# Sixteen pairs in three buffers, TensorE's products placed by time per slot, GpSimd's sums spaced, and the chunk loop written out

## The reference, cut to what matters

```python
xc, z = jnp.split(jnp.einsum('bld,ed->ble', x, W_in), 2, axis=-1)
u = silu(conv1d(xc, w_c) + b_c)                                  # 1024 channels, 4 taps
dt, Bm, Cm = jnp.split(jnp.einsum('bld,ed->ble', u, W_x), [32, 48], axis=-1)
delta = softplus(jnp.einsum('blr,dr->bld', dt, W_dt) + b_dt)
A = -jnp.exp(A_log)                                              # 1024 x 16
h[t] = exp(delta[t] * A) * h[t-1] + delta[t] * Bm[t] * u[t]      # 16 states per channel
y[t] = (h[t] * Cm[t]).sum(states) + u[t] * Dp
out = jnp.einsum('bld,od->blo', y * silu(z), W_out)
```

## Time and profile before

| | us |
|---|---|
| median of 3 runs | 8613.19 (8611.42 to 8617.14) |
| the profiled execution | 8617.45 |
| its span, first to last instruction | 8615.6 |
| first scan of chunk 0 | 238.9 |
| last scan's end | 7757.2 |

### The profile page before, as it was taken

How to read it: one execution, slowest core, us unless ns; L and a number is a source line. 1 busy time by engine, 2 the same in 40 slices (tenths; PEclk the granted TensorE clock), 3 DMA queues, 4 the chain that set the end, 5 groups by cost and what they waited for, 6 DMA issues and landing times. The chain is left out here.

```text
span 8615.6 us, 126403 instructions
## 1 busy us (share of the span) xinstructions
PE 7396.0 (86%) x31688; PEld 4113.0 (48%) x31688; DVE 7620.8 (88%) x8802; ACT 5873.9 (68%) x10702; POOL 6574.0 (76%) x2826
## 2 busy tenths in 40 slices
PE   5788888888888888888888888888888888876886
PEld 3444444444444444444444444444444444445753
DVE  2899999999999999999999999999999999995717
ACT  5777777777777777777777767777777777754415
POOL 0888888888888888888888888888888888881103
...
GB/s 197 49 51 50 46 50 51 51 51 52 53 51 47 51 52 49 45 63 61 61 51 52 51 52 46 51 51 48 46 50 51 51 52 50 47 37 153 166 127 148
DMA packets 223573, 552.99 MB, mean 64 GB/s; under 512 B 26272, under 2 KB 26528, under 8 KB 201824
## 3 DMA queue, kind: packets, MB, share of 16 engines
...
## 5 line engine op out<-in xcount | busy, mean ns | idle before, releaser
L931 POOL TENSOR_TENSOR bu<-w,b_rep 128x1024 f32<-128x1024 f32 x2048 | 4808.6, 2361 | 956.0 <-DVE h L1007 955.9
L1007 DVE TENSOR_TENSOR_SCAN h<-decay,h_last,bu 128x512 f32<-128x512 f32 x3840 | 4817.3, 1271 | 200.1 <-PE turn L519 140.6
L728 ACT ACTIVATE decay<-delta,neg_a 128x512 f32<-128x512 f32 x4096 | 2802.7, 689 | 1862.4 <-DVE h L1007 1848.1
L519 PEld LDWEIGHTS turn<-ident_m,h 128*128 128x128 f32 x16384 | 1918.4, 143 | 3163.2 <-DVE acc L1027 1246.1
L519 PE MATMUL turn<-ident_m,h 128*128 128x128 f32 x16384 | 2591.6, 282 | 615.3 <-DVE acc L1027 359.3
L1027 DVE SCALAR_TENSOR_TENSOR acc<-turn,c_now,acc 128x512 f32<-128x512 f32 x3200 | 2327.5, 727 | 191.9 <-PE turn L519 185.8
L448 PE MATMUL proj<-conv_in,conv_diag 128*128 128x512 f32 x2048 | 1039.7, 596 | 45.7 <-ACT halo L662 45.7
L448 PE MATMUL proj<-x_conv,w_in 128*128 128x512 f32 x2048 | 1055.5, 613 | 22.0 <-DMA x_conv<-xt 17.0
L448 PE MATMUL proj<-x_gate,w_in 128*128 128x512 f32 x2048 | 1034.2, 597 | 43.1 <-ACT stage L718 29.5
L448 PE MATMUL proj<-zy,w_out 128*128 128x512 f32 x2048 | 1033.7, 599 | 0.9 <-DVE zy L1036 0.9
L946 POOL TENSOR_TENSOR acc_v<-acc_v,prod 128x1024 f32<-128x1024 f32 x320 | 755.2, 2360 | 16.7 <-ACT prod L742 16.7
...
## 6 DMA issues: line engine op xcount, KB each, us to landing
b_rep<-b_rows SPq DMA_DIRECT2D x1024, 256.0 KB, 3.3
...
xt<-stage ACTq DMA_DIRECT2D x128, 256.0 KB, 2.4
...
```

What stands on the lines that cost most here:

```text
L519: mm = pe.transpose(out[:, b * P:(b + 1) * P], h[:, k % 2, b, j * P:(j + 1) * P], ident[:])
L728: act.activation(decay[:, b, :], delta[:, blk, :], ACT.Exp, scale=neg_a[:, n, blk:blk + 1]).then_inc(decay_set, 1)
L931: pool.tensor_tensor(bu[:, s // 2 % 4, :, :], w[:, blk:blk + 2, :], b_rep[:, k % 4, :].unsqueeze(1).to_broadcast([P, 2, T]), ALU.mult).the ...
L1007: dve.tensor_tensor_scan(h[:, k % 2, b, :], decay[:, b, :], bu[:, s // 2 % 4, b % 2, :], start, ALU.mult, ALU.add).then_inc(scanned, 1)
```

## The change

What it does, part by part:

- All 16 pairs go by ScalarE and GpSimd, in three buffers of `prod`. The buffer of the first pair of a half is the running total, so `acc_v` is gone. The first product of pair q waits for GpSimd's addition of the pair that had its buffer, in most cases q - 2.
- The products are laid out by time: each slot has the same total of weights, turn tiles included (state 0.55, skip 1.05, product 1, x_proj 1.1, delta 1.25). That is about 1.3 products in a slot with one state tile.
- The skip tiles move from slots 0 to 3 and 32 to 35 to slots 4, 5, 6, 7 and 30, 33, 36, 39, and the second half's y tiles from 20, 22, 24, 26 to 22, 24, 26, 28. `PROD_LAG` is 2 instead of 3.
- A Silu is moved to a position (`silu_at`) where no product follows it for some slots. The pieces between it and its half's last copy stay in list order.
- GpSimd's four sums and four products for `delta` and `w` stand at fixed positions 17, 21, 25, 29, 49, 53, 57, 61. Before, each product stood one position behind its sum.
- The loops over chunks become Python loops: every chunk is written out.

The diff, cut to its core:

```diff
-         ("conv", 7, 0), ("out", 0, 0), ("x_proj", 0, 0), ("turn_c", 0, 0), ("out", 1, 0), ("delta_next", 0, 0), ("out", 2, 0),
-         ("delta_next", 1, 0), ("out", 3, 0), ("delta_next", 2, 0), ("gate", 0, 0), ("delta_next", 3, 0)] + [
-         ("gate", b, 0) for b in range(1, NB)]
+         ("conv", 6, 0), ("conv", 7, 0), ("out", 0, 0), ("x_proj", 0, 0), ("turn_c", 0, 0), ("out", 1, 0), ("delta_next", 0, 0),
+         ("delta_next", 1, 0), ("out", 2, 0), ("delta_next", 2, 0), ("delta_next", 3, 0), ("out", 3, 0)] + [
+         ("gate", b, 0) for b in range(NB)]
-RATE = 1.17
-TAKE_LAG, TAPS_LEAD, W_LAG, X_PROJ_LAG, XDBL_LAG, CONV_LAG, PROD_LAG = 4, 2, 10, 5, 3, 4, 3
+TAKE_LAG, TAPS_LEAD, XDBL_LAG, CONV_LAG, PROD_LAG = 4, 2, 4, 4, 2
+W_AT = {17: ("sum", 2), 21: ("product", 2), 25: ("sum", 3), 29: ("product", 3),
+        49: ("sum_next", 0), 53: ("product_next", 0), 57: ("sum_next", 1), 61: ("product_next", 1)}
+Y_AT = ((116, 118, 120, 122), (22, 24, 26, 28))
+SKIP_AT = ((7, 4, 5, 6), (30, 33, 36, 39))
+WEIGHT = {"x_proj": 1.1, "delta": 1.25, "delta_next": 1.25, "turn_c": 0.5, "state": 0.55, "skip": 1.05, "y": 0.55}
+def silu_at(end):
+    at = end + TAKE_LAG
+    behind = (at - PROD_LAG - 5) % (2 * J)
+    return at if behind < 5 else at + 2 * J - behind
 def timetable():
-    at, end_of = 0.0, {}
+    room = [-sum(WEIGHT[tile[0]] for tile in tiles_at) for tiles_at in TURN_AT]
+    whole = sum(PRODUCTS[kind] * WEIGHT.get(kind, 1.0) for kind, _, _ in ORDER) - sum(room)
+    room = [r + whole / (SLOTS_BODY - 3) for r in room]
+    slot, left, end_of = 0, room[0], {}
...
-        slots = [int(at + q / RATE) for q in range(PRODUCTS[kind])]
-        at += PRODUCTS[kind] / RATE
+        slots = []
+        for q in range(PRODUCTS[kind]):
+            while left < WEIGHT.get(kind, 1.0) / 2 or slot < earliest:
+                slot += 1
+                left = min(left, 1.0) + room[slot]
+            slots.append(slot)
+            left -= WEIGHT.get(kind, 1.0)
...
-V_PAIRS = [q for q in range(GROUPS // 2) if q % HALF_Q != 2]
-V_SET = {q: i % 2 for i, q in enumerate(V_PAIRS)}
+V_BUFFER = (0, 1, 2, 1, 2, 1, 2, 1, 2, 1, 0, 1, 0, 1, 0, 1)
+def emptied_before(q):
+    old = max(o for o in range(-len(V_BUFFER), q) if V_BUFFER[o] == V_BUFFER[q])
+    pair = old % len(V_BUFFER)
+    return ("join", pair // HALF_Q) if pair % HALF_Q == 0 else ("pair", pair), old < 0
...
-        with eng.Fori(start + 1, end) as G:
+        for G in range(start + 1, end):
             run(G, Kind(layer))
...
-    prod = sb("prod", [P, 2, 2, HB * P])
-    acc_v = sb("acc_v", [P, 2, HB * P])
+    prod = sb("prod", [P, 3, 2, HB * P])
...
-            more = prod[:, 1 - V_SET[q]] if q % HALF_Q == 1 else acc_v[:]
-            pool.tensor_tensor(acc_v[:], more, prod[:, V_SET[q]], ALU.add).then_inc(vsum_set, 1)
+            total = prod[:, V_BUFFER[q - q % HALF_Q]]
+            pool.tensor_tensor(total, total, prod[:, V_BUFFER[q]], ALU.add).then_inc(vsum_set, 1)
```

More of the change, by code:

```diff
@@ L107 @@
+LAST_SKIP = [("skip", hf, SKIP_AT[hf].index(max(SKIP_AT[hf]))) for hf in range(2)]
 TURNS = 2
@@ L125, in turn_tiles, with timetable @@
     return order, carried
 TURN_AT, CARRIED = turn_tiles()
+WEIGHT = {"x_proj": 1.1, "delta": 1.25, "delta_next": 1.25, "turn_c": 0.5, "state": 0.55, "skip": 1.05, "y": 0.55}
[3 more added lines that the diff above has]
+    return at if behind < 5 else at + 2 * J - behind
+def timetable():
+    room = [-sum(WEIGHT[tile[0]] for tile in tiles_at) for tiles_at in TURN_AT]
+    whole = sum(PRODUCTS[kind] * WEIGHT.get(kind, 1.0) for kind, _, _ in ORDER) - sum(room)
+    room = [r + whole / (SLOTS_BODY - 3) for r in room]
+    slot, left, end_of = 0, room[0], {}
+    work, take = [[] for _ in range(SLOTS_BODY)], [[] for _ in range(2 * SLOTS_BODY)]
+    for i, (kind, x, earliest) in enumerate(ORDER):
+        if kind == "conv":
+            earliest = end_of["conv_half", x] + CONV_LAG
+        if kind == "x_proj":
+            earliest = silu_at(end_of["conv", NB - 1]) + 1
+        if kind in ("turn_c", "delta_next"):
+            earliest = end_of["x_proj", 0] + XDBL_LAG
+        slots = []
[5 more added lines that the diff above has]
+            left -= WEIGHT.get(kind, 1.0)
+        for at in sorted(set(slots)):
+            lo = slots.index(at)
+            work[at].append((kind, x, i, lo, lo + slots.count(at)))
+        end = end_of[kind, x] = slots[-1]
+        if kind == "conv_half":
+            take[end + TAKE_LAG - TAPS_LEAD].append(("taps", x, i))
+        take[end + TAKE_LAG].append((kind, x, i))
+        if kind.startswith("delta") and x % 2 == 1:
+            for q, part in enumerate(("exp", "ln")):
+                take[end + TAKE_LAG + 1 + q].append((part + kind[5:], x // 2, i))
+        if kind == "conv" and x % HB == HB - 1:
+            take[silu_at(end)].append(("silu_u", x // HB, i))
+        if kind == "gate" and x % HB == HB - 1:
+            take[silu_at(end)].append(("silu_z", x // HB, i))
+    return work, take, end_of
@@ L129, with tiles @@
+WORK, TAKE, END_OF = timetable()
+def tiles(first, last):
+    kept = [i for i, (kind, _, _) in enumerate(ORDER) if not (first and kind in NOT_FIRST or last and kind in NOT_LAST)]
+    return {i: n for n, i in enumerate(kept)}, len(kept)
+PROJ_TILES, PROJ_FIRST = tiles(False, False)[1], tiles(True, False)[1]
+PROJ_PROLOGUE = 2 * NB + 1 + 1 + HB
 V_AT = (0, 3)
 HALF_Q = STATES // 2
-V_PAIRS = [q for q in range(GROUPS // 2) if q % HALF_Q != 2]
-V_SET = {q: i % 2 for i, q in enumerate(V_PAIRS)}
+SUM_LAG_Q = 11
@@ L135, in by_act @@
+V_BUFFER = (0, 1, 2, 1, 2, 1, 2, 1, 2, 1, 0, 1, 0, 1, 0, 1)
 def by_act(tile):
[L136 to L143 removed]
+    return tile[0] == "skip" or tile[0] == "state" and tile[2] == V_AT[tile[1] % 2]
+def emptied_before(q):
+    old = max(o for o in range(-len(V_BUFFER), q) if V_BUFFER[o] == V_BUFFER[q])
+    pair = old % len(V_BUFFER)
+    return ("join", pair // HALF_Q) if pair % HALF_Q == 0 else ("pair", pair), old < 0
@@ L432, in _ @@
             body(start, Kind(layer, at_start=True))
-            with sp.Fori(start + 1, end - 1) as G:
+            for G in range(start + 1, end - 1):
                 body(G, Kind(layer))
@@ L737, in product @@
                 act.wait_ge(c_set, 2 * G + (k // HALF_C + 1))
-            of_last, reader = reader_before(q)
-            if k % 2 == 0 and not (kind.first and of_last):
-                act.wait_ge(vsum_set, sum_base(G, kind) + (kind.sums.index(reader) + 1 + C_PROD))
-            act.activation(prod[:, V_SET[q], k % 2, :], turn[:, BANK[tile], :], ACT.Copy,
+            emptied, in_last = emptied_before(q)
+            if k % 2 == 0 and not (kind.first and in_last):
+                behind = in_last and emptied not in SUMS_CARRIED
+                at = SUMS.index(emptied) - len(SUMS) if behind else kind.sums.index(emptied)
+                act.wait_ge(vsum_set, sum_base(G, kind) + (at + 1 + C_PROD))
+            act.activation(prod[:, V_BUFFER[q], k % 2, :], turn[:, BANK[tile], :], ACT.Copy,
                            scale=c_now[:, j, n:n + 1]).then_inc(v_done, 1)
@@ L969, in body @@
             for p in range(PAIRS):
-                for what, pair in W_AT[p]:
-                    if kind.has(what.replace("sum", "delta").replace("product", "delta")):
-                        delta_w(G, what, pair)
+                what, pair = W_AT.get(p, ("", 0))
+                if what and kind.has(what.replace("sum", "delta").replace("product", "delta")):
+                    delta_w(G, what, pair)
                 k, pr = divmod(p, 2)
```

74 lines of the change are left out of this document (16 added, 58 removed).

## The result

The kernel became slower, not faster: 8828.72 us (median of 4 runs, 8821.29 to 8832.35) against 8615.08 of the kernel before (4 runs, 8611.42 to 8617.14). The ratio is 1.0247, with a 95% interval from 1.0230 to 1.0265. I had forecast 8427 and a range from 8300 to 8535. The profiled execution took 8832.35 us.

A forecast was written before the change was run, and what follows sets the result against it. VectorE was taken as the engine with least room, busy 222.6 us per chunk. New chunk: 220.0 busy + 9.4 idle = 229.4 against 235.3; with the end chunks 187 us less than 8617.4, or 8427 as median; range 8300 to 8535.

The forecast's parts named there:

- The rival of the emptied buffer: ScalarE's product waits for GpSimd to empty its buffer, 14.4 us more idle per chunk; 8859 us, chance 0.05.
- its margin at 3.3 less a lag of 1.9: GpSimd's addition frees a buffer 3.3 us before ScalarE's product needs it, less GpSimd's lag of 1.9: no wait.
- Position 119: silu_z stands ahead of gate 4's copy ... 1.2: At position 119 silu_z delays gate 4's copy, so gate 6 starts late and scan 120 waits 1.2 us.
- a halved clock: Within the TensorE-bound rival: product-free slots 75 to 77 halve the clock, up to 3 us a chunk; centre 8585, chance 0.08.
- a low clock in mid-chunk: Sign that the forecast is wrong: TensorE's granted clock falls in the middle of a chunk; no size given.
- 0.87 us: TensorE's price for one product of two passes, used throughout the slot-by-slot walk.
- both ring waits: Slots 84 to 88 and 92 to 96: delta_next pieces hold the two proj banks, delaying out 2 and out 3; 1.9 us each.
- The list of stalls: Slot-by-slot walk of VectorE's waits in a chunk of the new order, summing to 9.9 us.
- its upper bound of 15 idle: VectorE's idle per chunk could reach 15 us if the late tiles knock on.
- 29 us by my rows: Chunk edges: writing out the loop gains nothing in layer 1 and 2.1 us in 14 chunks of layer 2.
- hardly a stall: Rival: the new order leaves VectorE idle only 1 to 6 us per chunk, centre 3.5; 8247 us, chance 0.13.
- the new order does nothing: Rival: old stalls only move, idle stays 11.4 us per chunk; 8487 us, inside the forecast's range, no separate chance.

The follow-up runs named there:

- deltas apart: Changed kernel with the four delta_next pieces back in their old places, an out between each two; 8758.04 us.
- both back: Changed kernel with the first half's Silu of z back at position 116 and the delta_next pieces in their old places; 8582.88 us.
- skips spaced: As both back, but skip tiles moved to slots 1, 4, 5, 6 and 33, 37, 41, 45; 8592.73 us.
- The filled gap: Changed kernel with one more product, which nobody reads, in each of slots 75, 76 and 77 of chunks 1 to 30; 8765.89 us.
- Silu_z back: Changed kernel with the first half's Silu of z at position 116 instead of 119; 8642.01 us.
- looped: Changed kernel with the hardware loops over chunks restored; 8880.75 us.
- pairs and loop: Kernel before with sixteen pairs in three buffers and its loops written out, all else old; 8516.64 us.
- the best version: As skips spaced, with x_proj's copy and turn_c two earlier and every proj piece taken three slots after its last product, not four; 8417.06 us.

## Why the prediction was wrong

**Right: the pairs, and for the changed kernel the buffers and GpSimd.** Alone, the pairs brought 8617.87 to 8536.95, 81 us where the sum had 30 x 2.6 = 78. ScalarE's products never wait for GpSimd in the changed kernel (waits after), and the spacing changed nothing that can be told. The rival of the emptied buffer, which gave 8859 and so came nearest to the measured time, was wrong in its mechanism for this kernel: the loss has another cause. But that the wait is nothing held only behind the other stalls. In deltas apart, both back and skips spaced, where VectorE is faster from slot 86 on, it is there, 91 or 92 times in an execution, up to 2.5 us long and 191, 142 and 141 us in all. I had put its margin at 3.3 less a lag of 1.9.

**The step that failed: "Position 119: silu_z stands ahead of gate 4's copy ... 1.2".** I followed what the moved Silu delays on ScalarE and in the `proj` ring, and did not ask who reads its result. The y tile's gate product at slot 116 does (one Silu covers all four blocks of the half), and it was 4.0 us too early for it. TensorE, left without work by the same wait, then ran at half clock, which made 2.5 of the 1.2 at slot 120. Moving this one step back is worth 187 us of the 402 between forecast and result. The 402 are 375 in chunks 1 to 30 (12.5 each), 21 in the two end chunks and 5 outside the chunks.

**The second error: the clock as a rival, at one place.** I gave a halved clock 0.08, at slots 75 to 77, and named a low clock in mid-chunk as a sign that I am wrong; the sign came. It falls there, and at four other places: where a ring wait leaves TensorE short of work (86, 94), behind the Silu wait (117), and in the stretch of slots 22 to 28, where y tiles take the place of products (25). In the last one the stall of slot 26 comes and goes with it: in chunks 16 to 22 the clock stays up there and the stall is absent. I had priced every product behind a wait at 0.87 us; several cost twice that, and 0.5 + 1.4 us became 1.60 + 3.11. The filled gap shows that a low clock costs in this way (63 us in all, 1.6 per chunk at the two places themselves); for slots 86 and 94 the deltas edit took away the ring wait and the low clock together (59 to 71 us). How they share it is seen where the clock stays up behind the same ring wait: 1.8 us instead of 4.7 at slots 94 to 96 (chunk 22 after), and 1.12 + 0.64 = 1.8 instead of 2.7 at slots 86 to 88 (chunk 6 of Silu_z back). So both ring waits were priced about right, at 1.9 each, and the term that failed there is the 0.87 us per product, which left no room for a lower clock.

**The list of stalls** was otherwise a fair guide: at slots 6, 8, 28, 32, 38, 40, 43, 48, 87 and 88 each lies within 0.3 of its forecast, 7.9 us measured for 6.8 forecast. The 87 is in part luck: I had its products at full clock, and four passes took 2.94 us there. The sum failed by what it left out, and its upper bound of 15 idle held only late tiles, not a reader too early or a slower clock.

**The loop** was 29 us by my rows; it is 14 in the old order and 52 in the new one. Rows of a looped kernel can't price an edge for another order: in the old one the stalls at the edge shrank by 1.7 us a chunk, and 1.3 of them came back at slots 62 to 64 with a low clock there. Why TensorE idles twice as long at the edges of layer 2 as at those of layer 1 in looped stays open. The Trainium skill (Runtime: NRT & Kernel Launch, section Instruction fetch mechanics) says that a taken branch to code that isn't already fetched forces a fetch; the idle of 2.20 and 2.43 us under issue agrees, and both measured values stay below the 101 us that all of the idle of the earlier trace rows on all edges would give.

**The end chunks** were to save 9 us and lost 12: chunk 0 ends with the same slots.

**Of the other rivals,** hardly a stall (8247) was far off. That the new order does nothing (8487) was too kind: compared with pairs and loop (8516.64), the new order as a whole does harm, 312 us. The even load per slot was not useless by itself, since the best version keeps it, but what it was worth alone was not measured.
